# Cross attention: queries stacked densely, each head's score matmul on its own 64 rows of the array

## The reference

```python
def _L0_xattn_ref(x, y, Wq, bq, Wkv, bkv, Wo, bo):
    q = x @ Wq + bq
    kv = y @ Wkv + bkv
    k, v = jnp.split(kv, 2, axis=-1)
    q = q.reshape(B, SQ, 16, 8).transpose(0, 2, 1, 3)
    ...
    attn = jnp.einsum('bhqd,bhkd->bhqk', q, k) * scale
    attn = jax.nn.softmax(attn, axis=-1)
    out = jnp.einsum('bhqk,bhkd->bhqd', attn, v)
    ...
x = x + _L0_xattn_ref(_layernorm(x, axis=-1), ctx_768, ...)
```

## Time and profile before

| what | us |
|---|---|
| median of 3 runs (lowest, highest) | 1873.82 (1869.31, 1875.78) |
| span of the profiled execution | 1871.2 |
| PE busy, share of the span | 1655.1, 88% |
| PE weight loads busy | 962.9, 51% |
| DVE busy | 1179.3, 63% |
| ACT busy | 859.6, 46% |
| POOL busy | 415.5, 22% |
| mean granted TensorE clock | 0.939 of full |

### The profile page before, as it was taken

How to read it: one execution, slowest core, us unless ns; L and a number is a source line. 1 busy time by engine, 2 the same in 40 slices (tenths; PEclk the granted TensorE clock), 3 DMA queues, 4 the chain that set the end, 5 groups by cost and what they waited for, 6 DMA issues and landing times. The chain is left out here.

```text
span 1871.2 us, 34901 instructions
## 1 busy us (share of the span) xinstructions
PE 1655.1 (88%) x11429; PEld 962.9 (51%) x11429; DVE 1179.3 (63%) x2634; ACT 859.6 (46%) x1294; POOL 415.5 (22%) x499
## 2 busy tenths in 40 slices
PE   2677776799998999999999997999999999499998
PEld 1343443244444444444444443788888888344443
DVE  4655532668676776768687783677667765355554
ACT  1333323166666656566666665333334333133443
POOL 4000002030201102030303001443343332033331
PEclk9878886699999999999999998999999999699999
DMA  4212112513132323232232210000000000000001
GB/s 112 64 38 65 37 35 78 96 69 54 35 76 46 93 46 93 46 93 46 71 55 74 50 16 8 2 1 0 0 0 0 0 0 1 6 16 21 21 21 34
DMA packets 87510, 75.69 MB, mean 40 GB/s; under 512 B 23700, under 2 KB 77364, under 8 KB 86452
## 3 DMA queue, kind: packets, MB, share of 16 engines
q1 hardware_dynamic: 87380, 73.96, 17.7%
HBM read 43.25 MB, written 30.42 MB: 39 GB/s over the span
## 5 line engine op out<-in xcount | busy, mean ns | idle before, releaser
L1152 DVE TENSOR_REDUCE b_chunk_max<-psum 128x1 f32<-128x400 f32 (+1 forms) x1024 | 545.3, 570 | 215.1 <-PE psum L1367 207.1
L1290 ACT ACTIVATE b_prob<-psum 128x1024 f32<-128x1024 f32 (+1 forms) x416 | 425.9, 1024 | 255.4 <-PE psum L1404 247.9
L1367 PE MATMUL psum<-k_stack,q_stack 128*128 128x400 bf16 (+1 forms) x1024 | 320.6, 347 | 30.0 <-DMA k_stack<-b_k_scratch 10.7
L1376 PE MATMUL psum<-b_prob,b_v_aug 128*32 128x256 f32 (+1 forms) x3328 | 267.9, 394 | 2.6 <-PE psum L1319 1.7
L1404 PE MATMUL psum<-q_stack,k_stack 128*128 128x256 bf16 (+1 forms) x1664 | 255.0, 276 | 16.2 <-issue 16.0
L1404 PEld LDWEIGHTS psum<-q_stack,k_stack 128*128 128x128 bf16 (+1 forms) x1664 | 146.5, 100 | 136.9 <-issue 71.6
L1367 PEld LDWEIGHTS psum<-k_stack,q_stack 128*128 128x128 bf16 x1024 | 100.0, 98 | 200.3 <-DVE b_chunk_max L1152 171.2
L2064 DVE TENSOR_TENSOR e_hg<-e_gl,e_gate 128x512 f32<-128x512 f32 x128 | 128.2, 1020 | 108.7 <-ACT e_gl L2045 74.6
L1695 ACT ACTIVATE c_prob<-psum,c_mneg 128x128 f32<-128x128 f32 x128 | 47.0, 368 | 229.6 <-DVE c_mneg L1636 229.6
L2045 ACT ACTIVATE e_gl<-psum,b1T 128x512 f32<-128x512 f32 x128 | 87.8, 687 | 139.8 <-PE psum L2092 114.3
L2079 PE MATMUL psum<-e_hg,e_w 128*128 128x512 f32 x256 | 131.9, 598 | 8.9 <-DVE e_hg L2064 8.9
(11 more groups left out here) (221 smaller groups left out, 2154.7 us busy)
## 6 DMA issues: line engine op xcount, KB each, us to landing
k_stack<-b_k_scratch SPq DMA_DIRECT2D x32, 600.4 KB, 10.3
b_k_scratch<-b_kparts SPq DMA_DIRECT2D x7, 1200.8 KB, 4.4
b_k_scratch<-b_kparts SPq DMA_DIRECT2D x7, 800.5 KB, 6.1
b_ctx<-in_ctx SPq DMA_DIRECT2D x8, 576.0 KB
e_w<-in_L_ffn_re_w SPq DMA_DIRECT2D x62, 64.0 KB, 1.8
a_scratch<-a_parts SPq DMA_DIRECT2D x16, 192.0 KB, 2.1
k_stack<-a_scratch SPq DMA_DIRECT2D x16, 192.0 KB, 4.7
q_stack<-b_q_scratch SPq DMA_DIRECT2D x32, 96.0 KB, 2.3
```

The lines of the kernel that those rows point to most:

```text
L1152: nc.vector.tensor_reduce(out=chunk_max[:, half, q, column4(hh), c:c + 1], in_=psum[:, 2 + u % 2, 0:w], axis=AX.X, op=ALU.max).then_inc(ma ...
L1290: nc.scalar.activation(prob[0:k, buf, :].rearrange("p (a c) -> p a c", a=2), psum[0:k, 4 + 2 * buf:6 + 2 * buf, :], ACT.Exp, scale=HD ** - ...
L1367: nc.tensor.matmul(psum[:, 2 + u % 2, 0:hi - lo], queries_of(qst, h, slice(q * P, q * P + P)), keys_of(kst, h, slice(lo, hi)), start=True, ...
L1376: last = nc.tensor.matmul(pv[32 * hh:32 * hh + 32, :], v_aug[0:k, kt, g * GH + hh, :], prob[0:k, buf, c:c + T], start=(kt == 0), stop=(kt ...
```

## The change

Cross attention gets a query stack of its own, `qd` (q_dense), with two heads per tile like the key stack: 8 tiles where `qst` has 16. Nothing clears it, and nothing reads the rows that are not written. Every score and unit matmul takes only its own head's rows, 50 (scores) or 48 (units, without the shift rows), and names its place in the array: rows 0 to 63 for heads of even number, 64 to 127 for odd ones. Columns, banks, order, waits and the number of matmuls and DMAs stay the same. `load_operand` and `store_m` write to consecutive tiles instead of every second one.

```diff
             qst=sb("q_stack", [P, H, T], BF16),
+            qd=sb("q_dense", [P, H // 2, T], BF16),
...
+def half_of(stack, h, cols, rows=NP * HD + 2):
+
+    return stack[64 * (h % 2):64 * (h % 2) + rows, h // 2, cols]
...
-        qst, kst, ident = t["qst"], t["kst"], t["ident"]
+        qst, kst, ident = t["qd"], t["kst"], t["ident"]
...
-                load_stack(sp, (qst, kst)[which], (q_scr, k_scr)[which], which, slice(4 * half, 4 * half + 4), done)
+                load_stack(sp, (qst, kst)[which], (q_scr, k_scr)[which], 1, slice(4 * half, 4 * half + 4), done)
...
-                        sp.dma_start(stack_rows(qst, 0, par, SHIFT_ROW + m, 1, slice(2 * g, 2 * g + 2)), mparts[2 * par:2 * par + 2, m, :])\
+                        sp.dma_start(stack_rows(qst, 1, par, SHIFT_ROW + m, 1, slice(2 * g, 2 * g + 2)), mparts[2 * par:2 * par + 2, m, :])\
...
-                nc.tensor.matmul(psum[:, 2 + u % 2, 0:hi - lo], queries_of(qst, h, slice(q * P, q * P + P)),
-                                 keys_of(kst, h, slice(lo, hi)), start=True, stop=True).then_inc(max_full, 1)
+                nc.tensor.matmul(psum[:, 2 + u % 2, 0:hi - lo], half_of(qst, h, slice(q * P, q * P + P), NP * HD),
+                                 half_of(kst, h, slice(lo, hi), NP * HD), start=True, stop=True,
+                                 tile_position=(64 * (h % 2), 0)).then_inc(max_full, 1)
...
-                                                  keys_of(kst, h, slice(n * P, n * P + k)),
-                                                  queries_of(qst, h, slice(0, T)), start=True, stop=True)
+                                                  half_of(kst, h, slice(n * P, n * P + k)),
+                                                  half_of(qst, h, slice(0, T)), start=True, stop=True,
+                                                  tile_position=(64 * (h % 2), 0))
```

## The result

The changed kernel takes **1914.0 us** (median of 5 runs, 1910.61 to 1935.29) against 1873.82: a ratio of **1.0232** with a 95% interval of [1.0184, 1.0279]. It is slower, clear of the noise, where 1.8% faster was forecast; whether by more than 2%, the interval leaves open. The profiled execution is the slowest of the five, with a span of 1933.5 us and a mean clock of 0.878 over the launch; the other four have 0.887 to 0.896. What it shows of the clock is therefore somewhat more than the median run lost.

A forecast was written before the change was run, and what follows sets the result against it. Cross attention was taken as bound by PE's streams in seven of 13 intervals and DVE's chain in six. Gains 34.4 + 6.8 + 13.0 + 1, less 2.3, 11, 5 and 4, gave 33 us: 1841 us, range 1812 to 1864.

The forecast's parts named there:

- The clock: Rival: PE streams less and drops to the lower level; a tenth of cross attention's steps costs 48 us, 1889 us; chance 0.04.
- Score pairs: Cross attention: score matmuls of two heads in different halves stream together, about 0.21 us less per step where PE bounds.
- unit pairs: Cross attention: two adjacent units stream together when both banks are free, 0.16 us less where PE's streams bound.
- DVE's chain: Intervals behind a third unit are set by DVE's reductions, hold no score matmul and stay at 1.84 to 1.86 us.
- First and second intervals: After a DVE chain, the first interval falls from 1.45 to 1.08 us; the next waits for DVE, 1.49.
- New boundaries: Changes between tile kinds around prep items drain the array, 0.09 us each; 11 us lost, bounds 0 and 15.
- The key load: Part 1: the key transfer does not get shorter, so 0.7 us in seven entries becomes DMA wait; 5 us lost.
- the 33 us: Total forecast gain over all terms, taken off the median to give 1841 us, -1.8%.
- ACT: Part 0: ACT also evacuates context, keys, queries and values and limits some intervals; 4 us lost, bounds 0 and 8.
- The halves do overlap: Against the rival that halves exclude each other, leaving only boundary costs: 1885 us; slower 0.09, cancelled 0.10.
- the rest of the stream time: Rival: DVE never holds PE in cross attention, so the whole saved stream time returns, 1766 us; chance 0.05.

The follow-up runs named there:

- e4: Changed kernel with every score and unit matmul on the lower half of the array, 48 or 50 rows, so none overlap: 2422.6 us.
- e14: Kernel before, without 64-row tiles, but even heads use 66 rows instead of 128 in cross attention: 1889.9 us, ratio 1.0077.
- e9: Changed kernel with all 64 rows of a half in score and unit matmuls instead of 50 and 48, added query rows zero: 1867.2 us.
- e12: Changed kernel with 64 rows and score pairs issued twice behind a third unit, but part 0 as in the kernel before: 1861.4 us, ratio 0.9929.

## Why the prediction was wrong

**What failed.** The forecast carried the upper clock level of before over to the changed kernel. The clock stood among the rivals at 0.04, with three errors in that paragraph. "Against it: the gaps stay well below a microsecond" is not so even of the kernel before, where PE is idle for 3.1 to 3.6 us at each of five edges of the loop and the clock falls at the end of each. And gaps are not enough to tell: e4 is idle for 16 of 1339 us in all, nearly all of it at these edges, and never leaves 1.2 GHz. The Trainium skill's advice (TensorE: Matmul & The Clock Gate, Why this matters for your kernels) to keep TensorE continuously busy is met by e4 between its edges, some 170 us at a time, and e4 stays at the lower level; the measurement decides. Second, "it streams less" saw only the time: e14 and e9 show that the rows a matmul uses weigh as well, which the 64-row tiles cut from 128 to 48 or 50. Third, the size: a tenth of the steps was put at 1.2 us each. An interval costs 0.61 or 0.78 us more at the lower level (1.89 for 1.28 on average, 2.63 for 1.85), but a third of the steps' time came there (284 of 854 us).

**What held.** Score pairs and unit pairs: 0.21 to 0.22 and 0.17 us, forecast 0.21 and 0.16. DVE's chain behind a third unit: 1.85 us, untouched. First and second intervals: 1.06 and 1.49. In a part without items but the two at steps 2 and 9, that makes 20.7 us for 13 steps against 21.8; the forecast was 1.2 us less before drains.

**New boundaries.** An item's interval in the changed kernel, 418.50 to 419.94 us, is 1.44 against 1.67 for the same step before (1119.77 to 1121.44; its end is in the earlier trace rows): 0.23 won of the 0.39 that the two pairs bring here. The item starts 0.27 after units that stream for 0.17, so the boundary costs 0.10, and the item and its way to the values take 0.06 more. I took 0.09 in all. The rule of the Trainium skill (TensorEngine Tiling (Array Packing), Key Properties) that a change of mode drains the engine agrees with these rows for 64-row tiles too.

```profile
418.50 0.64 PE L1383 MATMUL psum<-b_prob,b_v_aug 128*32 128x256 f32 x8
419.07 0.39 PE L1411 MATMUL psum<-q_dense,k_stack 50*128 50x256 bf16 x4
419.30 0.34 PE L1373 MATMUL psum<-k_stack,q_dense 48*128 48x400 bf16 x2
419.57 0.44 PE L1354 MATMUL psum<-ident,b_pvs 128*128 128x128 f32 x2
419.94 0.64 PE L1383 MATMUL psum<-b_prob,b_v_aug 128*32 128x256 f32 x8
```

**The key load.** The forecast was 5 us in seven waits; the waits of the changed kernel have 7.2 us in six:

```profile
PE psum L1373 <- DMA k_stack<-b_k_scratch: 5.2, 5, 1.8
PEld psum L1373 <- DMA k_stack<-b_k_scratch: 2.0, 1, 2.0
```

where the kernel before has 1.0 and 0.7 us, once each.

**The sum.** Even at the upper level the 33 us would not have come. The changed kernel has parts without any time at the lower one; these are one of each kind, parts 3, 0, 1 and 2 in the program's order, counted from one value group to another:

```profile
708.62:731.43 22.81, 19.48 (x200) 7.03 (x199) 18.65 (x40) 14.36 (x17) 1.00 (x2) 1.00 0.58 91
384.02:412.80 28.78, 24.89 (x227) 9.97 (x226) 19.78 (x46) 21.27 (x31) 14.01 (x16) 1.00 0.10 39
664.25:687.93 23.68, 20.73 (x212) 8.43 (x211) 17.05 (x35) 15.68 (x19) 2.20 (x5) 1.00 0.55 118
687.93:708.62 20.69, 18.34 (x194) 6.50 (x193) 17.61 (x37) 13.97 (x16) 0.00 (x0) 1.00 0.01 2
```

The same parts take 23.5, 28.6, 24.4 and 21.8 us before. That is 2.3 us less for four parts; the forecast comes to about 4 (32 us over 31 groups of 13 steps). The gain is there in part 2, which has two prep items, and is missing in part 0, where every step has one, so the terms for new boundaries and for ACT were too small; how it divides between the two is open. In part 3 the boundary shows by itself: the interval into step 6, with an output item, takes 2.65 us (2.31 before), 0.10 of that ahead of the item and 0.10 more from its start to the values. Over the whole of cross attention I estimate some 20 us from these parts in place of 33 (seven entries at 2.3, and about 4 in the last). The lower clock then took 64 + 20 = 84 us in the profiled execution for 265 us more at that level, 0.32 us for each. The intervals say the same: their 0.61 of 1.89 and 0.78 of 2.63 us are 0.30 to 0.32 of the time spent low. These are estimates; no run shows the changed kernel at the upper clock throughout. The nearest is e12.

**The other rivals.** The halves do overlap. DVE's chain kept the rest of the stream time from returning, as its low chance said. (That rival's sum counts 404 steps; the trace has 416, 17 of them without units. The difference is under 3 us.)
